# Attention over 1024 tokens: query quarters in the weighing, three score banks each way, one transpose of the maxima, and a new order on every engine

## The reference

```python
    q, k, v = (split(q), split(k), split(v))
    scale = 1.0 / jnp.sqrt(jnp.float32(HEAD_DIM))
    scores = jnp.einsum('bhqd,bhkd->bhqk', q, k) * scale
    attn = jax.nn.softmax(scores, axis=-1)
    ctx = jnp.einsum('bhqk,bhkd->bhqd', attn, v)
```

## Time and profile before

| | before |
|---|---|
| median of 3 runs | 4611.63 us (4611.0 to 4611.99) |
| the profiled execution, its own time | 4603.94 us |
| its span in the trace | 4601.8 us |
| PE busy in the span | 4219.3 us, 92% |
| DVE busy | 3251.8 us, 71% |
| ACT busy | 2756.9 us, 60% |
| mean granted TensorE clock | 0.962 |

### The profile page before, as it was taken

The page is one execution under the profiler, slowest core; times in us unless marked ns, Lnnn a source line. Parts: engine busy times, 40 slices in busy tenths (PEclk is TensorE's granted clock), DMA queues, the critical chain, the costliest instruction groups (busy, mean ns, idle before and its releaser), DMA issues. The chain is left out here.

```text
span 4601.8 us, 97548 instructions
## 1 busy us (share of the span) xinstructions
PE 4219.3 (92%) x32438; PEld 2861.6 (62%) x32440; DVE 3251.8 (71%) x5725; ACT 2756.9 (60%) x7139; POOL 1931.9 (42%) x1276
## 2 busy tenths in 40 slices
PE   4999967999953579999999999999999999999997
PEld 2455543555531347777777777777777777777776
DVE  2677752777766767777777777777777777777775
ACT  1577723577723146666666666666666666666664
POOL 2000010000000056666666666666666666666663
PEclk9899988899977789999999999999999999999999
DMA  4211112211101120011100210011001110111001
GB/s 122 57 41 46 40 27 81 58 43 43 40 19 38 46 85 20 20 34 45 39 17 22 58 39 18 22 49 51 17 20 48 45 26 17 40 39 41 15 22 46
DMA packets 100922, 183.85 MB, mean 40 GB/s; under 512 B 24804, under 2 KB 58240, under 8 KB 100096
## 3 DMA queue, kind: packets, MB, share of 16 engines
q1 hardware_dynamic: 99712, 176.12, 14.3%
q0 software_dynamic: 768, 2.10, 0.2%
HBM read 99.52 MB, written 25.17 MB: 27 GB/s over the span
## 5 line engine op out<-in xcount | busy, mean ns | idle before, releaser
L610 DVE TENSOR_REDUCE maxima<-PS 128x1 f32<-128x512 f32 x1024 | 660.3, 687 | 242.6 <-PE PS L493 232.1
L1426 POOL TENSOR_TENSOR swp<-raw,table 128x512 f32<-128x512 f32 x384 | 481.3, 1274 | 635.8 <-DVE ss L1837 635.6
L1509 PE MATMUL PS<-wqk,xT 128*128 128x512 f32 x1536 | 688.0, 601 | 6.1 <-DMA wqk<-in_L_ffn_Wqkv 4.8
L590 ACT ACTIVATE probs<-PS 128x512 f32<-128x512 f32 x1024 | 551.8, 589 | 223.0 <-PE PS L509 218.5
L1456 POOL TENSOR_TENSOR probs<-probs,prob_recip 128x512 f32<-128x512 f32 x384 | 476.9, 1261 | 431.3 <-DVE prob_recip L1895 431.3
L1766 ACT ACTIVATE probs<-probs,neg 128x128 f32<-128x128 f32 x1536 | 597.1, 392 | 26.6 <-DVE neg L1889 25.1
L1436 POOL TENSOR_TENSOR rinv<-ssm,power 128x32 f32<-128x32 f32 x96 | 528.8, 5508 | 0.0
L493 PE MATMUL PS<-k_stack,q_stack 128*128 128x512 f32 x1024 | 466.6, 459 | 37.4 <-DMA k_stack<-L_attn_qk 17.7
L1509 PEld LDWEIGHTS PS<-wqk,xT 128*128 128x128 f32 x1536 | 284.3, 190 | 337.3 <-issue 254.1
L1612 PE MATMUL PS<-xnT,w 128*128 128x128 f32 x3840 | 477.6, 276 | 0.8 <-DVE hidden L1955 0.8
L482 POOL COPY v_head<-V 128x256 f32 (+1 forms) x64 | 25.4, 403 | 1041.7 <-PE PS L521 859.9
(11 more groups left out here) (231 smaller groups left out, 8567.1 us busy)
## 6 DMA issues: line engine op xcount, KB each, us to landing
V_window<-V SPq DMA_DIRECT2D x180, 256.0 KB, 2.9
wqk<-in_L_ffn_Wqkv SPq DMA_DIRECT2D x12, 1024.0 KB, 6.8
w<-in_L_ffn_W SPq DMA_DIRECT2D x18, 640.0 KB, 4.4
q_stack<-L_tok_qk SPq DMA_DIRECT2D x128, 80.0 KB
k_stack<-L_tok_qk SPq DMA_DIRECT2D x128, 80.0 KB
q_stack<-L_attn_qk SPq DMA_DIRECT2D x128, 80.0 KB
k_stack<-L_attn_qk SPq DMA_DIRECT2D x128, 80.0 KB
wv<-in_L_ffn_Wqkv SPq DMA_DIRECT2D x6, 1024.0 KB, 5.1
```

What stands on the lines that cost most here:

```text
L590: act.activation(probs[:, k % 8, :], ST(k % 2), ACT.Exp).then_inc(exp_done, 1)
L610: dve.tensor_reduce(maxima[:, par, k // 2, k % 2:k % 2 + 1], SM(k % 2), AX.X, ALU.max).then_inc(sm_maxed, 1)
L1426: pool.tensor_tensor(swp[:, w, :, a:a + LD // 2], raw[:, w, :, b:b + LD // 2], table[:, j % 2, 2 + w, a:a + LD // 2].rearrange("p (o d) -> ...
L1509: mm = pe.matmul(wide(kind, half, j), xT[:, k, at:at + P], rhs, start=(k == 0), stop=(k == DC - 1))
```

## The change

The ring of stacks grows from four heads to six. The banks for either kind of scores grow from two to three each (six of the eight banks). `weigh` now gives the four groups of the array the four query quarters of the same key tile: eight matmuls of 256 columns in place of four of 512, with four groups in a head as before. The groups then need no adding: `turn_output` turns the 128 x 256 result by two transposes of 128 x 128, once in a head. The maxima of all eight query tiles are turned by one transpose into eight rows of 128, ACT copies these 8 x 128 to `neg_row`, and a DMA puts them into row 0 of `qs`. The engines work on up to five heads at once, each with its lag, in an order that is written out per engine. A step holds the same 32 score matmuls as before.

```diff
-            sp.dma_start(c.group_sum[:, :], c.ins["group_sum"]).then_inc(ident_ready, 16)
...
-RING = 4
+RING = 6
...
-    GROUP = 4
+    QUARTERS = 4
+    QW = SEQ // QUARTERS
+    BANKS = 3
     vh = c.sb(ctx, "v_head", [P, RING, QT, VW])
-    probs = c.sb(ctx, "probs", [P, 8, CH])
-    maxima = c.sb(ctx, "maxima", [P, 2, QT, 2])
+    probs = c.sb(ctx, "probs", [P, QT, SEQ])
+    maxima = c.sb(ctx, "maxima", [P, QT, HALVES])
     neg_max = c.sb(ctx, "neg_max", [P, 2, QT])
-    partial = c.sb(ctx, "partial", [P, 2, CH])
-    recip = c.sb(ctx, "recip", [P, 2, GROUP])
-    SM, ST, O = (lambda i: c.PS[:, i, :]), (lambda i: c.PS[:, 2 + i, :]), (lambda i: c.PS[:, 4 + i, :])
-    MR, CB = c.PS[0:1, 6, :], c.PS[:, 7, 0:GROUP * VW].rearrange("p (g v) -> p g v", g=GROUP)
+    neg_row = c.sb(ctx, "neg_row", [QT, 2, P], F32R)
+    partial = c.sb(ctx, "partial", [P, 2, QW])
+    recip = c.sb(ctx, "recip", [P, QT])
+    O, CB, MR = c.PS[:, 6, 0:QW], c.PS[:, 7, 0:QW], c.PS[0:QT, 7, QW:QW + P]
+    def SM(r, k):
+        return c.PS[:, (r + k) % BANKS, :]
+    def ST(r, k):
+        return c.PS[:, BANKS + (r + k) % BANKS, :]
...
+        with eng.Fori(1, ITERS // RING) as turn:
             for u in range(RING):
-                step(turn * RING + u, u)
-        for it in range(ITERS - RING, ITERS):
-            step(it, it % RING)
+                step(turn * RING + u, u, turn)
+        for t in range(ITERS // RING * RING, ITERS + last):
+            step(t, t % RING, t // RING)
...
+            def place_row(h):
+                it, r, turn = h
+                sp.wait_ge(row_taken, it + 1)
+                sp.dma_start(qs[0:1, r, :].rearrange("o (a t) -> o a t", a=QT).bitcast(F32),
+                             neg_row[:, r % 2, :].bitcast(F32)).then_inc(row_loaded[r], 16)
+            def step(t, u, turn):
+                h0, h2 = (stage(t, u, turn, lag) for lag in (0, 2))
+                if h2:
+                    place_row(h2)
+                if h0:
+                    load(h0)
+            over_heads(sp, step, 2)
...
+            def max_row(h):
+                it, r, turn = h
+                pe.wait_ge(max_ready, it + 1)
+                misc_free(pe, "row", it)
+                pe.transpose(MR, neg_max[:, r % 2, :], c.ident[:, :]).then_inc(row_done, 1)
+            def score(h, k):
+                it, r, turn = h
+                if k == 0:
+                    pe.wait_ge(row_loaded[r], 16 * turn + 16)
+                wait(pe, exp_done, UNITS * it + k - BANKS + 1)
+                pe.matmul(ST(r, k), ks[:, r, (k // 2) * P:(k // 2 + 1) * P], qs[:, r, (k % 2) * CH:(k % 2 + 1) * CH],
-            def weigh(it, r, grp):
+            def weigh(h, grp):
+                it, r, turn = h
-                for j in range(4):
-                    kt = 4 * (grp % 2) + j
-                    mm = pe.matmul(O(half)[VW * j:VW * (j + 1), :], vh[:, r, kt, :], probs[:, 4 * (grp % 2) + j, :],
-                                   start=(grp % 2 == 0), stop=(grp % 2 == 1))
+                    wait(pe, o_taken, it)
+                for kt in (2 * grp, 2 * grp + 1):
+                    for j in range(QUARTERS):
+                        mm = pe.matmul(O[VW * j:VW * (j + 1), :], vh[:, r, kt, :], probs[:, kt, j * QW:(j + 1) * QW],
+                                       start=(kt == 0), stop=(kt == QT - 1))
-            def sum_groups(it, half):
-                for i in range(4):
-                    mm = pe.matmul(CB[:, i, :], partial[:, half, i * P:(i + 1) * P], c.group_sum[:, :],
+            def turn_output(h):
+                it, r, turn = h
+                pe.wait_ge(o_taken, it + 1)
+                misc_free(pe, "turn", it)
+                for i in range(2):
+                    mm = pe.transpose(CB[:, i * P:(i + 1) * P], partial[:, r % 2, i * P:(i + 1) * P], c.ident[:, :])
+                mm.then_inc(turned, 1)
+            def step(t, u, turn):
+                h0, h1, h2, h3, h4 = (stage(t, u, turn, lag) for lag in (0, 1, 2, 3, 4))
+                if h1:
+                    score_for_max(h1, 11)
...
+                if h2:
+                    score(h2, 0)
+                if h0:
+                    score_for_max(h0, 0)
+                    score_for_max(h0, 1)
+                if h3:
+                    weigh(h3, 2)
+                if h2:
+                    score(h2, 1)
+                if h0:
+                    score_for_max(h0, 2)
+                if h2:
+                    score(h2, 2)
+                if h1:
+                    max_row(h1)
+                if h0:
+                    score_for_max(h0, 3)
+                if h2:
+                    score(h2, 3)
+                if h0:
+                    score_for_max(h0, 4)
+                if h2:
+                    score(h2, 4)
+                if h0:
+                    score_for_max(h0, 5)
+                if h3:
+                    weigh(h3, 3)
+                if h0:
+                    score_for_max(h0, 6)
...
+            def take_row(h):
+                it, r, turn = h
+                act.wait_ge(row_done, it + 1)
+                if not isinstance(it, int) or it >= 2:
+                    act.wait_ge(row_loaded[(r - 2) % RING], 16 * (turn if r >= 2 else turn - 1) + 16)
+                act.activation(neg_row[:, r % 2, :], MR, ACT.Copy).then_inc(row_taken, 1)
+            def take_output(h):
+                it, r, turn = h
+                act.wait_ge(pv_done, 4 * it + 4)
+                wait(act, turned, it - 1)
+                act.activation(partial[:, r % 2, :], O, ACT.Copy).then_inc(o_taken, 1)
...
+            def row_maxima(h):
+                it, r, turn = h
+                dve.wait_ge(sm_maxed, UNITS * it + UNITS)
+                wait(dve, row_done, it - 1)
+                dve.tensor_reduce(neg_max[:, r % 2, :], maxima[:, :, :], AX.X, ALU.max, negate=True).then_inc(max_ready, 1)
+            def invert(h):
+                it, r, turn = h
+                dve.wait_ge(turned, it + 1)
+                wait(dve, ctx_done, it)
+                view = CB.rearrange("p (c g v) -> p c g v", c=2, g=QUARTERS)
+                dve.reciprocal(recip[:, :].rearrange("p (c g o) -> p c g o", c=2, g=QUARTERS), view[:, :, :, HD:HD + 1]).then_inc(ctx_recip, 1)
+            def finish(h):
+                it, r, turn = h
+                dve.wait_ge(ctx_recip, it + 1)
+                view = CB.rearrange("p (c g v) -> p c g v", c=2, g=QUARTERS)
+                out = context[:, :, bass.ds(it * HD, HD)].rearrange("p (g c) d -> p c g d", c=2)
+                by = recip[:, :].rearrange("p (c g o) -> p c g o", c=2, g=QUARTERS).to_broadcast([P, 2, QUARTERS, HD])
+                dve.tensor_tensor(out, view[:, :, :, 0:HD], by, ALU.mult).then_inc(ctx_done, 1)
```

More of the change, by code:

```diff
@@ new lines, in attend, with misc_free @@
+    MISC_JOBS = [("row", 1), ("turn", 4)]
+    MISC_TAKEN = {"row": row_taken, "turn": ctx_done}
+    def misc_free(pe, kind, it):
+        at = [k for k, _ in MISC_JOBS].index(kind)
+        t = it + MISC_JOBS[at][1]
+        for back in range(1, 4):
+            k, lag = MISC_JOBS[(at - back) % 2]
+            before = t - (0 if at >= back else (1 if at + 2 >= back else 2)) - lag
+            if not isinstance(it, int) or 0 <= before < ITERS:
+                wait(pe, MISC_TAKEN[k], before + 1)
+                return
@@ new lines, in over_heads, with stage @@
+    def over_heads(eng, step, last):
+        for t in range(RING):
+            step(t, t, 0)
+        with eng.Fori(1, ITERS // RING) as turn:
+            for u in range(RING):
+                step(turn * RING + u, u, turn)
+        for t in range(ITERS // RING * RING, ITERS + last):
+            step(t, t % RING, t // RING)
+    def stage(t, u, turn, lag):
+        if isinstance(t, int) and not 0 <= t - lag < ITERS:
+            return None
+        return t - lag, (u - lag) % RING, (turn if u >= lag else turn - 1)
@@ L467, in _, with load @@
         def _(sp):
-            def step(it, r):
+            def load(h):
+                it, r, turn = h
                 wait(sp, st_done, UNITS * (it - RING) + UNITS)
@@ new lines, in exponential, with step @@
+            def exponential(h, k):
+                it, r, turn = h
+                act.wait_ge(st_done, UNITS * it + k + 1)
+                if k % 4 == 0:
+                    wait(act, pv_done, 4 * (it - 1) + k // 4 + 1)
+                act.activation(probs[:, k // 2, (k % 2) * CH:(k % 2 + 1) * CH], ST(r, k), ACT.Exp).then_inc(exp_done, 1)
+            def step(t, u, turn):
+                h0, h1, h2 = (stage(t, u, turn, lag) for lag in (0, 1, 2))
+                if h0:
+                    take_row(h0)
+                if h1:
+                    exponential(h1, 3)
+                    exponential(h1, 4)
+                if h2:
+                    take_output(h2)
+                if h1:
+                    exponential(h1, 5)
+                    exponential(h1, 6)
+                    exponential(h1, 7)
```

(25 more changed lines are left out.)

210 lines of the change are left out of this document (93 added, 117 removed).

## The result

The changed kernel takes 4466.49 us (median of 4 runs, 4466.06 to 4469.18), the kernel before 4611.32 beside it (4 runs, 4608.69 to 4611.99): ratio 0.9688, 95% interval 0.9671 to 0.9705, 144.8 us less. Predicted were 4480, in a range of 4462 to 4532.

What follows compares the result with a forecast made beforehand. PE's own stream was taken as the bound: a step of 14.96 us falls to 12.70, 70.9 us less per attention, 3.4 more for constants, 0.4 less for a DMA: 4468.5 us; plus 7.7 and 4 gives 4480, range 4462 to 4532.

Steps and rivals of the forecast that it cites:

- PE's stream as the pace: In the attentions PE's own instruction stream sets the time, 14.96 us a head, while DVE and ACT keep up.
- The step: PE's work per head in the full attentions falls from 14.96 to 12.70 us: scores, weighings, maxima transpose and output.
- rival 1: In the weighing, added waves wait for their weights: 0.86 us a head, 4530 us, chance 0.06.
- The banks: Three score banks remove PE's short waits of 0.16 us a head; at worst these stay.
- Fill and drain: Start and end of each attention: 27.2 us plus 1 for the low clock, then 26.5 us.
- rival 3: PE's clock stays low beyond the fill: 12.7 us more in each attention, 4505 us, chance 0.08.
- The row's DMA and the loads: In each step both stay hidden behind PE's work, the next heads' loads with 1.8 us to spare.
- Rival 2: A chain between engines sets the attentions' pace: a step of 13.5 us, 4526 us, chance 0.17.
- POOL's constants: Larger `qs` and `ks` zeroing ahead of each projection holds `bqs` to 13.9 us: 3.4 us more in each attention.
- The sum: Whole kernel: 4468.5 us for the profiled run, 4476 as median, 4480 with 4 us for small waits.
- Rivals 1, 4 and 5: In order: exposed weight loads, 4530 us, chance 0.06; weighing matmuls not abreast, 4706, 0.04; PE not the bound, 4615, 0.02.

Runs made afterwards that it cites:

- 1: Changed kernel with the transpose of the maxima issued eight times in place of once: 4516.88 us.
- 2: Changed kernel with weighings streaming 128 of 256 columns, output copy and transposes on those alone: 4361.0 us, a step of 10.84 us.
- 3: Changed kernel with two more maxima a head on DVE, reading two score banks a second time: 4473.62 us.
- experiment 10: Changed kernel with the weighing's two loops exchanged, both key tiles of a query quarter directly in succession: 4467.32 us.
- 5: Changed kernel with PE's two kinds of scores in strict turns, three banks kept: 4466.81 us.
- experiment 6: Changed kernel with PE's two kinds of scores in strict turns and two banks of either kind: 4598.82 us, a step of 14.40 us.
- 4: Changed kernel with two score banks of either kind in place of three, bunched order kept: 4649.84 us, a step of 15.37 us.
- 11: Changed kernel with one wait added, so POOL sets its long constants only after DVE has written `bqs`: 4444.71 us.

## Why the prediction was right, and where its steps were not

**PE's stream as the pace: right.** Added transposes cost their full time (1), halved weighings gave it all back (2), and DVE took 1.3 us more a step for nothing (3).

**The step: 12.70 predicted, 12.54 measured.** A weighing takes 1.00 for 1.01, its edges some 0.10 and 0.11 as reckoned. The transpose of the maxima was put at 0.18 and costs 0.03 and an edge of 0.08 on the next score (0.31 for 0.23); the output was put at 0.28 and costs 0.14 and the same edge. 0.07 and 0.06 less; the other 0.03 lie in the weighings and in readings of two digits. The 0.86 a step of rival 1 did not show: the sixteen loads of a weighing, 0.11 us each, lie in the first 0.59 of its 1.00 us (301.57 to 302.16), beside its own matmuls, and a weighing with half as many loads took 0.99 before. Nor does a matmul wait until one for a busy group, ahead of it in the program, has started: in experiment 10 four starts lie within 0.04 us, in a weighing of 1.02.

**The banks: the number right, the reason wrong.** The step in the prediction was "I take the 0.16 as gone; at worst they stay". In the changed kernel they are gone. But "at worst they stay" priced the third bank at 0.16 us. By experiments 5 and 6 it is worth 14.40 - 12.54 = 1.86 us a step, 54 us an attention, three quarters of the whole gain when it comes last. Taking instructions from PE with two banks brings 14.96 - 14.40 = 0.56, though the count says 2.4. The reason is in the runs: I read the 0.16 as what two banks cost, when it was what they cost with a break after every fourth score; the change takes those breaks away. A bound for it could have been had from the rows of before: a maximum is begun 0.5 us after its score (305.20 to 305.74) and takes 0.69, while PE in turns comes back to the same bank after four scores, 0.92. The bunched order costs another 0.97 a step with two banks and nothing with three (4 to 6).

Nor were the 0.16 all waits. The timeline of the kernel before, behind the transposes of the maxima:

```profile
306.90 0.40 PE L509 MATMUL PS<-q_stack,k_stack 128*128 128x512 f32 x1
307.14 0.45 PE L493 MATMUL PS<-k_stack,q_stack 128*128 128x512 f32 x1
307.43 0.40 PE L509 MATMUL PS<-q_stack,k_stack 128*128 128x512 f32 x1
```

Here one score lasts 0.29 where 0.23 is the rule, and the others of this half head show no such gap: some 0.1 us a head. The rest lies within what two digits leave out in 32 scores.

**Fill and drain.** The first weighing starts 27.4 us after the first score (28.2 predicted), the drain takes about 27.7 (26.5). With 29 steps, a few of them 12.65, an attention is 419.4 and 418.8 us for 423.0. The clock was at the lower level for 19.3 us, 0.72 in the next 8 and then full, so rival 3 didn't come.

**The row's DMA and the loads: right.** The DMA of the row is issued at 301.18, the next eight loads from 302.14 to 305.27, the score that needs the row starts at 310.15 and the one that needs the loads at 310.38, with no wait ahead of either. Rival 2 didn't come, and at 10.84 us a step (2) PE was still the bound.

**POOL's constants: right.** 13.91 us for `bqs` as predicted. What the prediction did not ask is what the whole of it costs: 21.8 us, which one wait gives back (11).

**The sum.** 4468.5 predicted for the profiled run, 4466.1 measured. The 13.5 us between 4480 and the median are nearly all in the last two additions: 7.7 for the distance between a profiled run and its median, which was 0.4 this time, and 4 for small waits, of which there were none. That the profiled run came out within 2.4 us is in part luck: the attentions came out 6.4 us shorter than predicted, the stretches ahead of them 1.7 longer and the rest 2.4 longer. And the third bank, worth 108 us when it comes last (58 x 1.86), was in the change by its design and not by the sum: with two banks the prediction's own terms give 4480 + 58 x 0.16 = 4489 us, and experiment 6, which is that kernel in strict turns, took 4599. Rivals 1, 4 and 5 are refuted by the 1.00 us of a weighing and by experiment 1.

## What to carry to other kernels

Short waits for a buffer in a trace are the price of that depth in that order (0.16 us a head in the kernel before, 1.86 a step in experiment 6): before taking instructions out of a queue, count how many of its pieces stand between two breaks now and after, and hold that against the reader's latency. A cut on the pacing engine can be worth little without a deeper ring and much with it (0.56 and 2.42 us a step here). The third bank alone in the kernel before was not run; its rows leave at most 0.16 us a head for it. And an instruction of two elements a partition that takes ten microseconds is worth a look, whatever the change was about.

## What the runs showed of the hardware

- Matmuls for four different column groups run abreast whatever their order in the program: 1.00 us with the groups in turn, 1.02 with two matmuls of one group directly behind one another. In experiment 10 four starts lie within 0.04 us. Two waves of 512 columns take 0.99, four of 256 take 1.00, four of 128 take 0.57.
- A break costs by being there: a score ahead of a weighing lasts 0.32 and the one behind it 0.34 where 0.23 is the rule, and so does, at 0.34, a score that has waited for its bank (307.33 to 307.67).
- The clock: granted at 0.50 through 19.3 us of the fill in which PE was never idle by its records, though DVE set its pace (busy for 18.33 of them), and at 1.00 from 155.25 on.
- DVE's `bqs`, two elements a partition, took 13.91 and 15.69 us while POOL worked through its constants, not one of which is longer than 5.21 us; it ended with the last of them (61.29 and 61.26; in the second projection 617.18 and 617.16). Behind POOL's wait it took 0.23. DVE's subtraction of 128 x 512 (`low`, at 50.31 in experiment 11) ran in 0.69 us beside one of the same constants (`V`, 48.04 to 51.41). Why `bqs` was held up until POOL's last constant, and `low` not at all, no trace here shows.
